# Inverse square roots by one guess, a third-order step and a Newton step, in a transformer block on one NeuronCore

## What is computed

```python
def _layernorm(x, w, b, eps=EPS):
    m = jnp.mean(x, axis=-1, keepdims=True)
    v = jnp.mean(jnp.square(x - m), axis=-1, keepdims=True)
    return (x - m) * jax.lax.rsqrt(v + eps) * w + b
...
q = l2norm((h @ Wq).reshape(B, T, H, D))        # t * rsqrt(sum(t*t) + 1e-12)
k = l2norm((h @ Wk).reshape(B, T, H, D))
v = _layernorm((h @ Wv).reshape(B, T, H, D), vnw, vnb)
u = i_gate * k * v
_, mem = jax.lax.associative_scan(combine, (g, u), axis=1)
out = (_layernorm(mem, mnw, mnb) * q).reshape(B, T, C)
...                                              # a second norm per head, a gate
h = x + out @ Wo
h2 = _layernorm(h, ln2w, ln2b)
mlp = jax.nn.silu(h2 @ Wgate) * (h2 @ Wval) @ Wout
...
x = x + _layernorm(attention_part(_layernorm(x)))
x = x + _layernorm(experts_part(_layernorm(x)))  # 8 experts, top 2, and a shared one
```

## Time and profile before

| | |
|---|---|
| median of 3 runs | 619.25 us (618.31 to 620.9) |
| span of the profiled execution | 617.5 us |
| the profiled execution's own time | not given apart from its span |
| TensorE busy | 530.9 us, 86% |
| VectorE busy | 410.8 us, 67%, 1249 instructions |
| ScalarE busy | 261.6 us, 42% |
| GpSimd busy | 111.8 us, 18% |
| mean granted TensorE clock | 0.923 |

### The profile page before, as it was taken

The page is one execution under the profiler, slowest core; times in us unless marked ns, Lnnn a source line. Parts: engine busy times, 40 slices in busy tenths (PEclk is TensorE's granted clock), DMA queues, the critical chain, the costliest instruction groups (busy, mean ns, idle before and its releaser), DMA issues.

```text
span 617.5 us, 8177 instructions
## 1 busy us (share of the span) xinstructions
PE 530.9 (86%) x2464; PEld 419.4 (68%) x2464; DVE 410.8 (67%) x1249; ACT 261.6 (42%) x465; POOL 111.8 (18%) x133
## 2 busy tenths in 40 slices
PE   2844358999659999999999998999998989999991
PEld 1423135577546677887678786888886889999870
DVE  6786744779874699885488793341839656766447
ACT  4720355616364524266531435311144556666304
POOL 1510003200001404001305000022005114444400
PEclk9976778999767999999899999699998989999997
DMA  8970100001010003021001010001007224454263
GB/s 287 422 204 3 33 2 0 1 0 35 34 34 1 0 2 104 1 68 35 0 1 69 2 35 34 1 26 44 34 1 265 61 61 123 121 139 122 77 258 136
DMA packets 29549, 44.42 MB, mean 72 GB/s; under 512 B 3211, under 2 KB 24203, under 8 KB 29163
## 3 DMA queue, kind: packets, MB, share of 16 engines
q1 hardware_dynamic: 24515, 32.95, 16.8%
q0 software_dynamic: 3408, 9.38, 4.1%
q10 hardware_dynamic: 1584, 1.57, 0.9%
HBM read 27.55 MB, written 16.34 MB: 71 GB/s over the span
## 4 chain that ended last, share of the span: by engine, by line
PE 69%; DVE 20%; ACT 5%; issue 2%; DMA 2%; POOL 0%; ACTq 0%; POOLq 0%; DVEq 0%; SPq 0%
PE psum L765 14%; PE psum L724 12%; PE psum L725 12%; PE psum L726 12%; PE psum L791 6%; PE psum L840 3%; PE psum L734 3%; PE psum L812 2%; PE psum L826 1%; DVE XC L1214 1%; PE psum L915 1%; PE psum L932 1%; PE psum L962 1%; DVE rt L1001 1%; DVE rt L1000 1%
## 5 line engine op out<-in xcount | busy, mean ns | idle before, releaser
L634 ACT ACTIVATE SM<-psum 128x512 f32<-128x512 f32 (+1 forms) x56 | 33.1, 595 | 132.9 <-PE psum L726 94.9
L1340 DVE TENSOR_TENSOR SM<-SM,psum 128x512 f32<-128x512 f32 (+1 forms) x56 | 38.2, 682 | 45.8 <-ACT SM L634 45.4
L510 POOL DMA_INDIRECT x_dispatched<-XN,dest x32 | 34.8, 1087 | 167.2 <-DVE XN L1408 158.7
L765 PE MATMUL psum<-WOU,SM 128*128 128x256 f32 x256 | 60.0, 379 | 0.2 <-DVE SM L1340 0.2
L791 PE MATMUL psum<-WQKV,HT 128*128 128x512 f32 (+1 forms) x128 | 53.0, 568 | 6.1 <-ACT QKV L569 2.7
L501 POOL TENSOR_TENSOR OG<-QKV,hvec 128x256 f32<-128x256 f32 x16 | 13.3, 834 | 237.2 <-ACT IG L576 220.0
L765 PEld LDWEIGHTS psum<-WOU,SM 128*128 128x128 f32 x256 | 48.2, 189 | 10.8 <-issue 3.4
L519 POOL DMA_INDIRECT y_routed<-GO,g_dest x39 | 37.9, 971 | 64.2 <-ACT GO L699 63.4
L791 PEld LDWEIGHTS psum<-WQKV,HT 128*128 128x128 f32 x128 | 27.4, 220 | 29.6 <-issue 23.6
L765 PE MATMUL psum<-SDN,SM 128*128 128x256 f32 (+1 forms) x192 | 45.0, 383 | 0.0
L765 PEld LDWEIGHTS psum<-SDN,SM 128*128 128x128 f32 (+1 forms) x192 | 36.1, 191 | 7.0 <-issue 1.3
(11 more groups left out here) (285 smaller groups left out, 1350.7 us busy)
## 6 DMA issues: line engine op xcount, KB each, us to landing
XG<-x_dispatched SPq DMA_DIRECT2D x39, 130.0 KB, 2.6
YF<-y_routed SPq DMA_DIRECT2D x4, 1024.0 KB, 9.0
RUPR<-rup SPq DMA_DIRECT2D x1, 2816.0 KB
X<-x SPq DMA_DIRECT2D x4, 512.0 KB, 6.3
x_after_attention<-X SPq DMA_DIRECT2D x4, 512.0 KB, 2.8
QKV<-x ACTq DMA_DIRECT2D x3, 512.0 KB, 3.6
y_shared<-SH SPq DMA_DIRECT2D x3, 512.0 KB, 2.9
SHF<-y_shared SPq DMA_DIRECT2D x1, 1536.0 KB
```

The costliest lines, as they stand in the source:

```text
L510: nc.gpsimd.indirect_dma_start(XD[:, :], bass.IndirectOffsetOnAxis(dest[:, i, old + j:old + j + 1], 0), XN[:, j, :], None).then_inc(dispat ...
L634: nc.scalar.activation(SM[0:rows, g % 3, 0:tb], p_pair(n)[0][0:rows, 0:tb], ACT.Silu).then_inc(silu_ready, 1)
L765: last = nc.tensor.matmul(p_down[:, j // 2, (j % 2) * D:(j % 2 + 1) * D], SM[0:rows, g % 3, j * P:(j + 1) * P], weight[0:rows, m, :], star ...
L1340: nc.vector.tensor_tensor(SM[0:rows, g % 3, 0:tb], SM[0:rows, g % 3, 0:tb], value_rows(n, rows)[:, 0:tb], ALU.mult).then_inc(hid_ready, 1)
```

## The change

`guess` becomes one instruction: the argument's bits are read as an integer, multiplied by -0.5 and added to the constant. `halley` is a new third-order step of four instructions, which takes the place of the first two Newton steps. One Newton step follows as before. In `rs` the first half now ends with the guess; the third-order and the Newton step stand in the second half. Nothing else is changed: `PLACE`, `ORDER` and all buffers are the same. The lines of the changed kernel are numbered up to nine higher.

```diff
+HALLEY_Z, HALLEY_C = math.sqrt(0.375), 1.25 / math.sqrt(0.375)
...
             def guess(a, y):
 
-                link(nc.vector.tensor_scalar(y.bitcast(I32), a.bitcast(I32), 1, None, ALU.logical_shift_right))
-                step(nc.vector.tensor_scalar(y.bitcast(I32), y.bitcast(I32), -1.0, float(0x5F3759DF), ALU.mult, ALU.add))
+                step(nc.vector.tensor_scalar(y.bitcast(I32), a.bitcast(I32), -0.5, float(0x5F3759DF), ALU.mult, ALU.add))
+
+            def halley(a, y, t):
+
+                settle()
+                link(nc.vector.tensor_tensor(t, y, y, ALU.mult))
+                link(nc.vector.scalar_tensor_tensor(t, t, HALLEY_Z, a, ALU.mult, ALU.mult))
+                link(nc.vector.scalar_tensor_tensor(t, t, -HALLEY_C, t, ALU.add, ALU.mult))
+                step(nc.vector.scalar_tensor_tensor(y, t, 1.875, y, ALU.add, ALU.mult))
...
             def rsqrt(out, a, y, t):
 
                 guess(a, y)
-                for i in range(2):
-                    step(newton(a, y, t, y))
+                halley(a, y, t)
                 return newton(a, y, t, out)
...
                         settle()
                         guess(a, y)
-                        step(newton(a, y, t, y))
                     else:
-                        step(newton(a, y, t, y))
+                        halley(a, y, t)
                         newton(a, y, t, rr[:, 0:nj, HEADS:]).then_inc(rr_ready, 1)
```

## The result

| | before | changed |
|---|---|---|
| median of 4 runs | 619.64 us (618.31 to 620.9) | 609.33 us (608.32 to 609.73) |
| profiled execution | span 617.5 us | 608.32 us, span 605.9 us |
| TensorE's mean granted clock | 0.923 | 0.931 |

The ratio is 0.983 with a 95% interval of [0.981, 0.985], so 10.6 us faster [9.5, 11.6]; the forecast was 8.1 us. A later job (kernels measured one after the other on one chip) gave 606.53 us for the same changed kernel against 619.14 us, 12.7 us faster [10.9, 14.5]. The first lies in the forecast's range (608.0 to 614.8), the second 1.5 us under it. Why the gain is larger than the sum, and not the same twice, is the main question of the experiments.

A forecast was written before the change was run, and what follows sets the result against it. TensorE, busy 86% of the span, bounds the kernel; VectorE's roots pay only where it waits. Block 0's 3.67, blocks 1 to 3's 3.24 and the end's 1.20 us sum to 8.11, from 619.25 to 611.1 us; range 608.0 to 614.8.

The forecast's parts named there:

- `rs` of block 1: Block 1: root 0.91 us shorter, but TensorE waited only 0.68 us for its product, so 0.68 us.
- `x2` and `ln2` before 184 us: 158 to 184 us: two 4-column roots in series, 1.18 us, capped by ScalarE's XTH before HN at 0.93 us.
- `rs` of block 2: Block 2: root 0.91 us shorter, of which TensorE's wait was 0.83 us, so 0.83 us.
- `rs` and SM of block 3: Block 3: SM's product moves forward past three operations; TensorE had waited 0.21 us for it, so 0.21 us.
- Price of a removed operation: Each root on VectorE: a removed operation saves its duration plus a 0.035 us gap; 0.60 to 0.91 us per root.
- Removed operations aren't cheap: Rival denied here: removed operations cost just the 0.08 us between independent starts, gain 3.2 us, 616.0 us; chance 0.05.
- Hold-up in block 0: Block 0's rs root: GpSimd's work also holds up floating L1000, so the step saves 0.98 us, not 1.31.
- Seventeen roots worth nothing: 17 of 30 roots, mostly in blocks 1 to 3, lie under TensorE's work and give nothing.
- a rival, tied to the stage from 158 to 184 us: 158 to 184 us: shorter idle stretches keep the clock at 2.4 GHz, half of 8.1 us regained, 607.1 us; chance 0.06.
- Only bare stretches: Rival: only block 0 and the end give their gain, 4.87 us, 614.4 us; chance 0.16.
- Clock lost in blocks 2 and 3: Rival: TensorE idles in blocks 2 and 3, clock falls, up to 16.2 us lost, 627.3 us; chance 0.02.
- A hold-up of another kind: Rival: a step is held up by something new, leaving the time near no change; chance 0.05.

The follow-up runs named there:

- the pair above: Second profile of the kernel before (span 617.0 us) and first profile of the kernel with the short root only at the 13 places forecast on the path.
- its 13 roots: Against the kernel before, short root only at the 13 places forecast on the path, old root at the other 17: 606.58 us, repeated 606.67 us.
- the kernel with the 17 hidden roots: Against the kernel before, short root only at the 17 places forecast under other work: 616.80 us, ratio 0.9966.
- those seven roots alone: Against the kernel before, short root only in block 0 (ln0, rs, both rstd, ln2) and at the two final places: 615.07 us, ratio 0.993.
- the split table: Against the changed kernel, last eight operations of the last block's group table moved behind VectorE's multiply of SM: 605.13 us, ratio 0.978.

## Why the prediction was right, point by point

The first result lies in the range and its direction and mechanism were right, but that it lies there is partly luck: the shortened paths account for 8.6 of the 10.6 us, and the rest is a term that the sum didn't have.

The steps of its sum beside what TensorE's starts show, from the pair above (further places of the same two traces for blocks 2 and 3):

| term | forecast | shown | what else was in it |
|---|---|---|---|
| `ln0` of block 0 | 0.60 | 0.60 | |
| `rs` of block 0 | 0.98 | 0.91 | L1000 ends 1.38 us behind the guess's start, L993 had ended 1.32 us behind L992's |
| two `rstd` | 1.50 | 0.79 + 0.83 | the second beside 0.78 us of lower clock under VectorE's cover |
| `ln2` of block 0 | 0.59 | 0.60 | 0.50 us of clock ahead of it (4.23 - 3.13 = 1.10) |
| `rs` of block 1 | 0.68 | 0.79 | the wait's 0.67, and 0.12 behind it (0.84 against the group just ahead) |
| `x2` and `ln2` before 184 us | 0.93 | 0.61 + 0.48 | |
| `rs` of block 2 | 0.83 | 0.91 | |
| `rs` and SM of block 3 | 0.21 | 0.38 | |
| `x2` of block 3 | 0.59 | 0.53 | |
| the two final roots | 1.20 | 1.20 | 11.58 - 10.38 us in the first pair of profiles |
| **sum** | **8.11** | **8.63** | |

**Price of a removed operation.** Right: the rows have the same durations and spacing, and the kernel with three operations put back loses the gain again, within 1.7 us. Removed operations aren't cheap (that rival had 616.0 us). The estimate from the table of the Trainium skill (VectorE: DVE Perf Modes, "The TRN2 errata"), some 4.1 us in all, is refuted by the first pair already: 8-column operations take 0.17 us and start 0.20 us apart.

**Hold-up in block 0.** Right. L1000 took 0.71 us as its second row suggested, and moving GpSimd's work away brought it to 0.29. This case agrees with the Trainium skill (SBUF — State Buffer, "Who interferes with whom") for L1000, which reads two SBUF inputs. The guess has one input and was held up too, 0.64 against 0.23 us. Of the page's two conditions only the other one, a two-port mode, can apply to it, and the page counts `tensor_scalar` among the operations that can enter one. That the guess, left alone, takes 0.23 us where a two-input operation of as many columns takes 0.29 fits this; no run here shows the mode itself.

**The terms.** `rs` of blocks 1 and 2 was capped at the wait, and more came out, 0.79 and 0.91: the group also starts closer behind the one ahead of it on TensorE than with a wait. For `ln2` of block 1 the cap by ScalarE was the right limit, but it gave 1.09 instead of 0.93 us: HN starts at 173.76, 0.12 us before XTH's recorded end (172.79 + 1.09), so the gap that I took off is an overlap. SM in block 3 gave 0.38 for 0.21 us. With the 0.06 us too much for `x2` these mis-sized terms come to 0.5 us.

**Seventeen roots worth nothing.** Right: the change and its 13 roots are equal in the same job, 606.53 and 606.67 us, and TensorE's starts agree up to 281 us.

**The rest, 2 to 4 us, is what the sum left out.** The paths give 8.6 us; the jobs measured 10.6 and 12.7 us. The step that failed is that the clock entered only as a rival, tied to the stage from 158 to 184 us. That stage did little: its clock rose from 0.69 to 0.71, and the rival's 607.1 us, half of its loss won back, isn't what happened, though the half-clock stretch that begins in it and reaches beyond 184 us is 3.4 us shorter, which gave some 1.2 us.

Most of the surplus is in the full stages, but not in the same ones in each profile. In the first pair (the spans of 617.5 and 605.9 us, 3.0 us beyond the roots) some 0.6 us comes up ahead of 221 us, and 1.7 us between 378 and 398 us, where the granted clock was 0.63 and is now 0.76 at the same busy time:

```profile
384.00:398.00 14.00, 11.99 (x47) 10.43 (x46) 3.59 (x9) 6.97 (x10) 0.00 (x0) 0.63 0.11 37
```

```profile
376.00:390.00 14.00, 11.99 (x53) 10.35 (x51) 4.98 (x15) 6.98 (x10) 0.00 (x0) 0.76 0.11 39
```

Behind 451 us that pair gains 0.1 us: the changed kernel has the late stretches there as well. In the pair above 1.7 us of it comes up between 221 and 448 us, where only the kernel before has a half-clock stretch (3.5 us of work near 295 us), and 2.9 us behind 451 us, where it has two (near 475 and 496 us) that the other lacks. Ahead of 200 us the clock gave 0.5 us and took 1.0. That makes 4.1 of the 4.2 us by which the two spans (617.0 and 604.2) differ beyond the roots. The changed kernel's second profile (span 607.5), the slowest run of its job, has only 0.9 us beyond them against the same 617.0. So the surplus goes from 0.9 to 4.1 us with the execution, at the same roots on the path.

What stays open: why the changed kernel loses less to such stretches at the median; its own two profiles hardly have fewer of them, and neither is of a run near the later job's median. With 2 and 3 us of delay the stretches near 287, 464 and 485 us are absent, with 1 us they are all there. Both late ones are absent too in the kernel with the 17 hidden roots, in which no group of TensorE lay more than 0.7 us from its place in the first profile before, up to 381 us. But two executions of one kernel differ as well, so a cause isn't shown. No experiment here could hold the clock fixed. A forecast of this kernel should have carried a term for it, by these profiles 1 to 4 us of gain. The range reached 3.1 us down, which held the first result (609.33) and missed the second (606.53).

**Rivals.** Only bare stretches: refuted, since those seven roots alone give 4.5 us and the change 10.6. Clock lost in blocks 2 and 3: TensorE is busy 25.00 of 25 us there at a clock of 1.00, as before. A hold-up of another kind: none shows in TensorE's starts, where every root of the table brings its lead.

## What to carry to other kernels

Price a shortened chain at its places: operations that wait for each other cost their duration and the gap, at each place little more than the wait behind it, and nothing under a busy engine. Here the forecast was 8.1 us and the traces show 8.6. Then look for short half-clock stretches in the stages where TensorE is full: here twelve matmuls took 4.4 us in one and 2.9 us outside, and whether one occurred differed between variants and between executions of one kernel. A gain of the size of one or two of them needs several executions' profiles and variants of the timing (a pure delay is the cheapest) before it is put down to the edit.

## What the runs showed that was not expected

- Delay was free here. With 2 us of idle work added at the start, the median stays within the changed kernel's two medians, and the profiled span is 603.1 us against 605.9 and 607.5.
- The same twelve matmuls behind the same 2.3 us wait take 2.9 us or 4.2 to 4.4 us. The wait doesn't decide: every profile here but that of the split table has it, thirteen in all. The clock falls to 1.2 GHz behind it in five (the kernel before twice, the first profile of the changed one, the seven bare roots, 1 us of delay) and holds in the other eight, the changed kernel's second among them.
- Taking work off VectorE under full cover (17 roots) made the kernel 2.1 us faster at the median of 11 runs; in its profile all of that is clock, and no cause of it is shown.
- GpSimd's 0.7 us operations held up even a one-input integer operation of VectorE, 0.64 for 0.23 us.
